# Half blocks of 64 rows in place of the last seven blocks of 128 of a mixture-of-experts layer, and GpSimd drains between its scatter-adds

## What is computed

```
x = x + xattn(layernorm(x), ctx)           # 16 heads, linear position bias
y = layernorm(x)                           # 2048 rows of 256
gate = softmax(y @ Wg + bg)                # 8 experts, the 2 largest are kept
w = top2(gate) / (sum(top2(gate)) + 1e-8)
for e in range(8):
    h = gelu(y @ W1[e] + b1[e])            # 256 -> 1024
    out += (h @ W2[e] + b2[e]) * w[:, e]   # 1024 -> 256
result = x + out
```

## Time and profile before

| what | us |
|---|---|
| three runs | 425.68, 430.43, 431.43 |
| median | 430.43 |
| span of the profiled execution, first to last instruction | 422.9 |

### The profile page before, as it was taken

One profiled execution on the slowest core, in us unless ns is written; L12 is line 12 of the kernel. 1 busy time (PEld: TensorE's weight loads), 2 busy tenths in 40 slices (PEclk: granted clock), 3 DMA queues, 4 the chain that ended last, 5 costly groups with the idle time before them and its releaser, 6 DMA issues.

```text
span 422.9 us, 15170 instructions
## 1 busy us (share of the span) xinstructions
PE 385.5 (91%) x4834; PEld 300.9 (71%) x4834; DVE 318.1 (75%) x989; ACT 217.8 (52%) x587; POOL 186.6 (44%) x273
## 2 busy tenths in 40 slices
PE   4868999999999989999999999999999999999960
PEld 3746777766677777777787877877787777778740
DVE  6576998979888877854788989776777777777760
ACT  2445786767777756645384444444443444444420
POOL 3300267777776666554543333233233333333341
PEclk9997999999999999999999999999999999999995
DMA  8648867777788654237233563332332333333210
GB/s 278 135 118 253 241 198 231 221 232 207 231 239 231 189 196 139 91 78 250 64 54 66 95 121 52 52 49 36 51 45 40 47 45 47 45 53 47 28 15 0
DMA packets 73441, 50.88 MB, mean 120 GB/s; under 512 B 48400, under 2 KB 67472, under 8 KB 73232
## 3 DMA queue, kind: packets, MB, share of 16 engines
q1 hardware_dynamic: 66168, 41.44, 36.1%
q0 software_dynamic: 7152, 8.47, 11.8%
q10 hardware_dynamic: 48, 0.01, 0.0%
HBM read 28.52 MB, written 17.37 MB: 109 GB/s over the span
## 4 chain that ended last, share of the span: by engine, by line
PE 63%; DVE 14%; issue 7%; POOL 6%; DMA 5%; ACT 1%; SPq 1%; ACTq 0%; DVEq 0%; POOLq 0%
PE ps L1264 59%; POOL rs L569 3%; DVE mx L925 3%; DVE wts L910 3%; DMA out<-stage,row_id 2%; POOL rs L571 2%; DMA area<-qd 2%; PE ps L1408 2%; PE ps L1402 2%; DVE xn L855 1%; DMA area<-in_x 1%; PE ps L1423 1%; DVE area L1179 1%; DVE nbT L1069 1%; DVE st L974 1%
## 5 line engine op out<-in xcount | busy, mean ns | idle before, releaser
L1264 PEld LDWEIGHTS ps<-stage,wts 128*128 x1872 | 130.8, 98 | 40.5 <-issue 2.0
L1264 PE MATMUL ps<-stage,wts 128*128 128x128 f16 x1872 | 155.2, 219 | 1.3 <-issue 1.3
L1264 PE MATMUL ps<-wts,area 128*128 x624 | 150.3, 327 | 0.1
L808 ACT ACTIVATE area<-ps,late 128x128 f32<-128x128 f32 x312 | 89.1, 371 | 114.5 <-PE ps L1264 111.5
L628 POOL DMA_INDIRECT out<-stage,row_id x39 | 69.0, 1770 | 129.7 <-DVE stage L1212 74.6
L1264 PE MATMUL ps<-area 128*128 128x128 f16 (+5 forms) x784 | 61.2, 226 | 6.8 <-DMA area<-qd 3.8
L1177 DVE TENSOR_SCALAR area<-area 128x512 f16<-128x512 f32 x78 | 33.7, 432 | 42.7 <-ACT area L808 39.6
L925 DVE TENSOR_REDUCE mx<-ps 128x3 f32<-128x462 f32 (+1 forms) x96 | 53.3, 577 | 12.8 <-PE ps L1264 12.8
L1264 PEld LDWEIGHTS ps<-area 128*128 128x128 f16 (+1 forms) x784 | 45.4, 101 | 18.5 <-issue 7.8
L1179 DVE SCALAR_TENSOR_TENSOR area<-area 128x512 f16<-128x512 f32 x78 | 54.8, 702 | 2.7
L671 ACT ACTIVATE area<-ps 128x512 f32<-128x512 f32 x80 | 47.0, 601 | 17.3 <-PE ps L1264 14.5
(11 more groups left out here) (131 smaller groups left out, 413.4 us busy)
## 6 DMA issues: line engine op xcount, KB each, us to landing
stage<-in_w SPq DMA_DIRECT2D x32, 512.0 KB
area<-qd SPq DMA_DIRECT2D x16, 256.0 KB, 4.0
qd<-wts SPq DMA_DIRECT2D x48, 64.0 KB, 2.1
area<-in_x SPq DMA_DIRECT2D x16, 128.0 KB, 3.3
out<-area SPq DMA_DIRECT2D x16, 128.0 KB
xlist<-pad_rows SPq DMA_DIRECT2D x15, 130.0 KB, 3.7
area<-nbT SPq DMA_DIRECT2D x64, 1.0 KB
area<-in_b SPq DMA_DIRECT2D x1, 1024.0 KB, 8.7
```

What stands on the lines that cost most here:

```text
L808: last = nc.scalar.activation(h32[par][:, c * P:(c + 1) * P], h_ps[par][m][:, f * P:(f + 1) * P], ACT.Gelu_apprx_tanh, bias=b1T[:, ds(numb ...
L1264: return nc.tensor.matmul(out_, lhsT, rhs, start=start, stop=stop, skip_group_check=skip)
```

## The change

Instead of 39 blocks of 128 rows there are NBLK = 36: 32 whole ones, of which LEFT = 15 lie in the second schedule, and four blocks (MIXED = 20, 23, 26, 29) which are made of NHALF = 7 half blocks of HP = 64 rows, two in each of the first three and one in the last. Each half has its own expert. The number of list entries that are loaded and added stays 32 + 7 = 39.

- `up`: in a mixed block each half is multiplied by its own expert's W1, with 64 moving columns: for two halves 48 matmuls per step instead of 24, at 32 different addresses instead of 16.
- `down_turned`: in a mixed block W2 is stationary and h moving (64 columns), so y comes out turned: per step 4 chunks x halves x 2 x 3 matmuls. `y_out` (ACT) adds the bias b2 and writes it to SBUF, `turned_back` (PE) transposes it back with two float32 matmuls, `weigh_turned` (DVE) scales it.
- `gelu_half`: one activation per half and slice in a mixed block.
- `load_block`, `add_block`: one load and one indirect DMA per half, one after the other; the gate values get eight slots instead of four (`ex_d` is awaited at t - 7 instead of t - 3), and SP reads the block's row number behind the waits instead of ahead of them.
- The second schedule on DVE has whole and half entries (16 ends instead of 8) and is spread over slots 14 to 27.
- POOL executes `pool.drain()` after the adds of blocks 3, 8, 13, 18, 22, 27, 31 and 33.

```diff
-NBLK = (2 * B * NQ - E) // P + E
-SPARE = NBLK - 2 * B * NQ // P
+HP = P // 2
+NFULL = 2 * B * NQ // P
+NHALF = E - 1
+NBLK = NFULL + (NHALF + 1) // 2
+SPARE = (NHALF + 1) // 2
...
+LEFT = NFULL - K1
+MIXED = (K1 + 3, K1 + 6, K1 + 9, K1 + 12)
+ENTRIES = NFULL + NHALF
...
+RETIRED = (3, 8, 13, 18, 22, 27, 31, 33)
...
+        def entries(t):
+            if t in MIXED:
+                first = NFULL + 2 * MIXED.index(t)
+                return list(range(first, min(first + 2, ENTRIES)))
+            return [t - sum(j < t for j in MIXED)]
...
             def add_block(t):
                 pool.wait_ge(s.y_done, t + 1)
-                wait(pool, s.added, 16 * t)
-                pool.indirect_dma_start(
+                for n in range(len(entries(t))):
+                    wait(pool, s.added, adds(t) + 16 * n)
+                    pool.indirect_dma_start(
...
             for t in range(2, NBLK):
                 add_block(t)
+                if t in RETIRED:
+                    pool.drain()
...
+            def y_out(t, e):
+                par, i = t % 2, MIXED.index(t)
+                act.wait_ge(s.y_ps_d, t + 1)
+                wait(act, s.yt_back, i)
+                for n, entry in enumerate(entries(t)):
+                    for dc in range(DC):
+                        at_ = dc * P + n * HP
+                        nc.scalar.activation(yT[:, at_:at_ + HP], y_ps[par][:, at_:at_ + HP], ACT.Identity,
+                                             bias=b2T[:, ds(number(e[entry]) * DC + dc, 1)], scale=1.0 / (S_H * SW)).then_inc(s.yt_d, 1)
...
             def up(k, f, w1e):
...
-                c8 = 4 * m + f
-                for c in range(DC):
-                    for a, z in THREE:
-                        last = mm(h_ps[par][m][:, f * P:(f + 1) * P], w1e[:, a, c * F + c8 * P:c * F + (c8 + 1) * P],
-                                  xT[t % 4][:, (2 * z + c) * P:(2 * z + c + 1) * P],
-                                  c == 0 and (a, z) == (0, 0), c == 1 and (a, z) == (1, 0))
+                c8, size = 4 * m + f, size_of(t)
+                for n, w in enumerate(w1e):
+                    for c in range(DC):
+                        for a, z in THREE:
+                            x0 = (2 * z + c) * P + n * size
+                            last = mm(h_ps[par][m][:, f * P + n * size:f * P + (n + 1) * size], w[:, a, c * F + c8 * P:c * F + (c8 + 1) * P],
+                                      xT[t % 4][:, x0:x0 + size], c == 0 and (a, z) == (0, 0), c == 1 and (a, z) == (1, 0))
...
+            def down_turned(k, f, w2e):
+                t, c, par = k // 2, 4 * (k % 2) + f, k // 2 % 2
+                if f == 0:
+                    pe.wait_ge(s.hh_lo, k + 1)
+                for n, w in enumerate(w2e):
+                    for dc in range(DC):
+                        for a, z in THREE:
+                            at_ = c * P + n * HP
+                            last = mm(y_ps[par][:, dc * P + n * HP:dc * P + (n + 1) * HP], w[:, (2 * c + a) * D + dc * P:(2 * c + a) * D + (dc + 1) * P],
+                                      hh_[par][:, z, at_:at_ + HP], (c, n, dc, a, z) == (0, 0, 0, 0, 0), c == FC - 1 and (a, z) == (1, 0), True)
+                if c == FC - 1:
+                    last.then_inc(s.y_ps_d, 1)
+
+            def turned_back(t):
+                par, n = t % 2, HP * len(entries(t))
+                pe.wait_ge(s.yt_d, adds_mixed(t))
+                for dc in range(DC):
+                    last = nc.tensor.transpose(y_ps[par][0:n, D + dc * P:D + (dc + 1) * P], yT[:, dc * P:dc * P + n], ident)
+                last.then_inc(s.yt_back, 1)
...
                 for f in range(4):
                     if ahead and k > 0:
                         up(k, f, w1e)
-                    if here:
-                        down(k - 3, f, w2e)
+                    if here and (k - 3) // 2 in MIXED:
+                        down_turned(k - 3, f, w2e)
+                    elif here:
+                        down(k - 3, f, w2e[0])
...
+                if k % 2 and (k - 5) // 2 in MIXED:
+                    turned_back((k - 5) // 2)
```

More of the change, by code:

```diff
@@ L539, in _ @@
                 load_block(t)
[L540 removed]
+            sp.wait_ge(s.added, adds(NBLK))
         @block.gpsimd
@@ L823, in _ @@
                 gelu_half(k, e)
+                if k % 2 == 0 and k // 2 - 2 in MIXED:
+                    y_out(k // 2 - 2, e)
                 if k == 4:
@@ new lines, in bases_of_half @@
+            def bases_of_half():
+                then(dve.scalar_tensor_tensor(out=bases[:, 1, 0:2 * E], in0=left[:, 1, :], scalar=float(P),
+                                              in1=s32[:, S_LIST:S_LIST + 2 * E], op0=ALU.mult, op1=ALU.add))
+                then(dve.scalar_tensor_tensor(out=bases[:, 1, E:2 * E], in0=single, scalar=-float(HP),
+                                              in1=bases[:, 1, E:2 * E], op0=ALU.mult, op1=ALU.add))
+                then(dve.scalar_tensor_tensor(out=bases[:, 1, 0:2 * E], in0=ends[:, 1, :], scalar=-float(HP),
+                                              in1=bases[:, 1, 0:2 * E], op0=ALU.mult, op1=ALU.add))
@@ L1059, in negated, with both_experts @@
+            def both_experts():
+                pairs = NHALF // 2 * 2
+                halves = sched_f[HP:P, 1, WORDS * FIVE + LEFT:WORDS * FIVE + LEFT + pairs].rearrange("p (n h) -> p n h", h=2)
+                then(dve.tensor_copy(halves[:, :, 0], halves[:, :, 1]))
             def negated(t):
@@ L1190, in extract @@
+                w = [wsel[tokens(t), slot, n:n + 1] for n in range(4)]
+                dve.tensor_scalar(w[0], zsum, 1e-8, 1.0, ALU.mult, ALU.add).then_inc(s.wa_d, 1)
+                dve.scalar_tensor_tensor(out=w[3], in0=first, scalar=sched_f[tokens(t), 1, column:column + 1], in1=z,
                                          op0=ALU.is_equal, op1=ALU.max).then_inc(s.we_d, 1)
                 dve.wait_ge(s.wa_d, t + 1)
-                dve.tensor_tensor(wsel[:, slot, 1:2], wsel[:, slot, 0:1], z, ALU.add).then_inc(s.wc_d, 1)
@@ L1193, in extract @@
-                wait(dve, s.added, 16 * (t - 3))
-                dve.tensor_copy(row_id[:, slot:slot + 1], pay[slot][:, 0:1].bitcast(i32)).then_inc(s.wb_d, 1)
+                dve.tensor_tensor(w[1], w[0], z, ALU.add).then_inc(s.wc_d, 1)
+                wait(dve, s.added, adds(t - 3))
+                of = pay[t % 8][:, 0:1].bitcast(i32)
+                if len(entries(t)) > 1:
+                    for n, skipped in enumerate((S_UPPER, S_LOWER)):
+                        dve.tensor_tensor(row_id[:, slot, n:n + 1], of, s32[:, skipped:skipped + 1], ALU.add).then_inc(s.wb_d, 1)
+                else:
+                    dve.tensor_copy(row_id[tokens(t), slot, 0:1], of[tokens(t)]).then_inc(s.wb_d, 1)
@@ L1221, in _ @@
                 if k == 2 * NBLK - 2:
-                    weigh(k // 2 - 2, number(e[k // 2 - 2]))
+                    weigh(k // 2 - 2, number(e[entries(k // 2 - 2)[0]]))
                 if k < 2 * NBLK:
@@ L1237, in _ @@
                         e = e + experts(dve, 1)
-                    weigh(k // 2 - 2, number(e[k // 2 - 2]))
+                    if k // 2 - 2 not in MIXED:
+                        weigh(k // 2 - 2, number(e[entries(k // 2 - 2)[0]]))
+                if k % 2 and (k - 5) // 2 in MIXED:
+                    weigh_turned((k - 5) // 2)
                 if k == 5:
@@ L1523, in _, with evacuated @@
                 turn(i)
+            def evacuated(t):
+                if t > 0 and t - 1 in MIXED:
+                    pe.wait_ge(s.y_done, t)
+                else:
+                    wait(pe, s.yb_d, 2 * full_before(t))
             def up(k, f, w1e):
@@ L1604, in _ @@
                 if ahead and k > 0:
-                    w1e = weights(e[k // 2])[:, 0:2, :]
+                    w1e = first(k)
                 if here:
```

283 lines of the change are left out of this document (193 added, 90 removed).

## The result

| | before | after |
|---|---|---|
| median (runs) | 429.23 us (4) | 446.56 us (4) |
| lowest to highest | 425.68 to 431.43 | 444.98 to 447.74 |
| span of the profiled execution | 422.9 | 444.6 |

Before has a fourth run here, of 428.02 us, beside the three that the forecast started from.

The account below looks back on a forecast made before the run. The prediction held PE to be bound by its array with its queue almost as full, at 0.13 us per new address. Terms -16.1 + 36.2 - 1 + 2 - 5.5 = +15.6 us on 430.4 gave 446.0 us, range 435 to 457.

Parts of the forecast that it names:

- three blocks fewer: Block loop: three blocks less at 5.38 us each, -16.1 us.
- addresses, six up steps: PE, up steps of the three two-half blocks: 36 addresses each, 4.68 us in place of 2.69; +11.9 us.
- addresses, six turned steps: PE, down steps of the three two-half blocks: 48 addresses each, 6.24 us in place of 2.69; +21.3 us.
- addresses, the single half: PE, last mixed block: up steps unchanged at 20 addresses, down steps 32 addresses, 4.16 us; +2.9 us.
- the queue's lead: PE's queue runs ahead of the array, a lead spent once when mixed blocks begin: -1 us (0 to -2).
- turning y back, waits for `weigh_turned`: PE, mixed blocks: float32 transposes, and a possible wait on DVE's scaling for the last one: +2 us (0.5 to 4).
- drains: POOL: time grows with indirect DMAs since the last drain, 0.08 us each; 5.87 us final drain shrinks to 0.3: -5.5 us.
- the last adds: POOL's scatter-adds, 39 before and after, were taken to cost nothing extra: 0 us.
- PE is bound by its queue: PE, mixed blocks: each new weight address takes 0.13 us in the instruction queue, +36.2 us in all; chance 0.66.
- The rival that went by that floor alone: PE, mixed blocks: the array is the bound and the queue hides its addresses; -21.6 us, 408.8 us; chance 0.11.
- Scatter-adds: 0: POOL: also 39 adds; two of one block follow each other but are needed only two blocks later; 0 us.
- The rival with a fixed price: POOL: every drain takes nearly 5.9 us, so the end keeps it and the tail loses about 2.5; 454 us; chance 0.18.

Follow-up runs that it names:

- experiment 5: Kernel before, with the second matmul of each down pair reading the low part of W2 at its own address: 464.15 us, ratio 1.0943.
- experiment 3: Changed kernel, with PE taking all weights of the mixed blocks from constant addresses (experts 0 and 1): 416.30 us, ratio 0.9724 to before.
- experiment 7: Changed kernel, with constant addresses in the turned downs of the mixed blocks only, ups unchanged: 422.89 us, ratio 0.9835 to before.
- experiment 6: Kernel before, with the weights of every block at constant addresses, so no register addresses for slices on PE: 422.14 us, ratio 0.9934.
- experiment 1: Changed kernel without the eight drains in POOL's loop: 450.15 us, ratio 1.0605 to before.
- experiment 8: Kernel before, with a single drain in the loop, behind the add of block 33: 423.86 us, ratio 0.9936.
- experiment 4: Kernel before, with the three products of an up ordered (high, high), (low, high), (high, low): 424.99 us, ratio 0.9997.

## Why the prediction was right, and where not

The steps, with the working of the prediction not repeated; measured values are from the two profiled executions:

| term | forecast | measured |
|---|---|---|
| three blocks fewer | -16.1 | -16.1 |
| addresses, six up steps | +11.9 | +12.6 |
| addresses, six turned steps | +21.3 | +21.5 |
| addresses, the single half | +2.9 | +2.9 |
| the queue's lead | -1 | 0 |
| turning y back, waits for `weigh_turned` | +2 | +3.5 |
| drains | -5.5 | -5.7 |
| the last adds | 0 | +2.8 |
| sum | +15.6 | +21.5 (spans: +21.7) |

How the right column comes out: an up step 4.79 - 2.69 (the mean of the first mixed block's two), six times; turned blocks 12.54 - 5.38, three times; the single half 8.25 - 5.38; the term of turning back is what is left of the loop's +24.4 us.

**PE is bound by its queue: right.** 1728 register instructions, steps of 4.8 and 12.5/2 us against the 4.7 and 6.2 forecast; 0.13 us per address is confirmed by experiment 5 (0.134), and its cause by experiments 3 and 7: with constant addresses the same matmuls run at the array's pace. The reported 46 ns is not the price, and experiment 5 shows the same. The prediction had this beside the Trainium skill (Perfetto Trace Analysis, Sequencer-only Instruction), by which such a window is the execution alone. The floor of about 25 ns for small matmuls that the Trainium skill gives (TensorE: Matmul & The Clock Gate, Back-to-back issue gap) is kept where addresses are constant: in experiment 7 twelve turned downs and six ups take 0.68 us, which leaves 0.029 for a turned down. The rival that went by that floor alone fell.

**The queue's lead: wrong, -1 us forecast, 0 found.** I had read it behind ten long downs. Experiment 6 shows that in the steady loop the queue is behind the array, so no lead stands at block 20: its first up step takes 4.78 us and its second 4.80. The most that a lead can have given anywhere in that block is the 0.3 us between its two turned steps, 6.12 and 6.43.

**Turning y back: right in kind, too small.** PE waited for `weigh_turned` in two places, and not only for the last mixed block. This is the first, in block 29's second up step, which waits for the y of block 26; idle time before the group in brackets:

```profile
388.82 0.50 PE L1445 MATMUL ps<-wts,area 128*128 x2
390.03 0.65 PE L1445 MATMUL ps<-stage,wts 128*128 128x64 f16 x6 [0.71 <-DVE stage L1365]
```

Blocks 28 and 31, in which the two waits fall, are longer by 1.1 and 0.9 us. The rest is 0.3 to 0.5 us per mixed block, of which the two transposes make 0.2 (start to start in the timeline). The term's bounds, 0.5 to 4, held it.

**The last adds: the step "Scatter-adds: 0" failed for the tail.** I had checked the adds only inside the loop. With 39 blocks the last ones are spare and their adds move nothing; with 36 the serial chain at the end has real rows. The last add is issued 7.0 us behind the last matmul instead of 5.1, and lands after 3.7 instead of 2.7. That the rows themselves make the landing longer is read from the two stretches above; it wasn't tried alone, and the longer distance from PE to the last issue has part of its cause in the same landings one block earlier. Another part may be the drains': without them (experiment 1) the last add is issued 6.5 us behind the last matmul instead of 7.0.

**Drains: right at the end, wrong in the loop, without effect.** The linear price is shown by the series above. But a drain in the loop doesn't take the 0.4 us of the forecast, nor the first one 3: they last 4.2 to 5.8 us. Their ends follow the landing of the add just issued, by some 0.2 us with two to seven DMAs and by 1.6 with the 36 of the first, so a drain waits for that add too. That costs nothing since POOL would wait for that landing anyway, and PE doesn't wait for POOL; experiment 8 shows what it costs when it lasts longer. The rival with a fixed price fell: it wanted 5.9 us at the end.

**The number.** 446.0 against 446.56 is closer than the sum deserves. The terms were 6 us short against the profiled executions, and the medians of before and after happen to lie 17.3 us apart where the ratio says 20.7.

## What to carry to other kernels

Count the different register-dependent operand addresses of a loop beside its columns: at 0.13 us each they are a second bound for PE, hidden only while the columns take longer. Cutting blocks into halves doubles them for the ups where it leaves the columns alone, and the turned form, with W2 stationary, takes those of the downs from 8 to 64. (Not tried: halves with h stationary would need only 16 for their downs, for twice the columns, an estimated 8 x (0.216 + 0.109) = 2.6 us more per block. These are the sizes of the two downs in the expectation of experiment 6, which its 5.28 us per block bear out.) GpSimd's drain at the end of this program costs 0.08 us for each indirect DMA since the last drain; drains inside the loop, where the queue waits for a landing anyway, take that off the end, and the kernel before gains 0.9% from them (0.6 to 1.2; 420.73 us, the fastest kernel here that leaves nothing out). Before blocks are taken away, look at what the last ones carry: empty ones can be a cushion for whatever is serial at the end.

## What the runs showed that I had not expected

- A slice's address costs the queue only when it is new: with the products in the order high, low, high there are 1560 register instructions as with high, high, low, and the same time, ratio 0.9997 (experiment 4).
- PE's array alone takes 5.28 us per block and the queue, by estimate, 5.36. The kernel before was bound by the queue by 0.1 us, although the page shows PE 91% busy (experiment 6).
- A drain behind an add whose transfer is in flight lasts 3.3 to 5.7 us with two to seven DMAs to retire, 5.8 to 7.1 with 36 (the first in the loop) and 7.7 with 66. It ends some 0.2 us after that add's landing in the first case, some 1.6 in the second and 3.3 in the third. That is less than 0.082 us for each DMA (3.0 and 5.4 us), so part of the price falls into the landing; how much of it can stays open.
- Without the addresses the mixed blocks meet the next bound at once, two adds per block, one after the other at 2.8 to 5.3 us each, and PE waits 7.5 us for DVE (experiment 3).
